# A two-layer decoder on one core: LayerNorm means moved into centred weights, scales into the evacuations, of the third many-head stage

## The reference, cut to what matters

```python
def _ln(x, g, b, eps=1e-05):
    m = jnp.mean(x, -1, keepdims=True)
    var = jnp.mean((x - m) ** 2, -1, keepdims=True)
    return (x - m) * jax.lax.rsqrt(var + eps) * g + b
def _proj(x, g, b, W, bias):
    return _ln(x, g, b) @ W.T + bias
...
qh = split_heads(_proj(q, ln_q_w, ln_q_b, w_q, b_q))
kh = split_heads(_proj(k, ln_k_w, ln_k_b, w_k, b_k))
vh = split_heads(_proj(v, ln_v_w, ln_v_b, w_v, b_v))
...
return _proj(o, ln_o_w, ln_o_b, w_o, b_o)
```

## Time and profile before

| what | us |
| --- | --- |
| median of 3 runs | 926.53 (925.84 to 928.22) |
| the profiled execution's own time | 924.71 |
| its span, first to last instruction | 922.9 |
| TensorE busy | 859.1 (93%) |
| VectorE busy | 549.8 (60%) |
| ScalarE busy | 423.1 (46%) |
| GpSimd busy | 234.9 (25%) |

### The profile page before, as it was taken

One profiled execution on the slowest core, in us unless ns is written; L12 is line 12 of the kernel. 1 busy time (PEld: TensorE's weight loads), 2 busy tenths in 40 slices (PEclk: granted clock), 3 DMA queues, 4 the chain that ended last, 5 costly groups with the idle time before them and its releaser, 6 DMA issues.

```text
span 922.9 us, 16788 instructions
## 1 busy us (share of the span) xinstructions
PE 859.1 (93%) x6416; PEld 703.1 (76%) x6416; DVE 549.8 (60%) x1371; ACT 423.1 (46%) x1226; POOL 234.9 (25%) x351
## 2 busy tenths in 40 slices
PE   3889999997999999999999998999989999999998
PEld 3777777775878888777777676777757888888887
DVE  2566777776322212777778776777755555555554
ACT  1335666655322232666665566666775312222211
POOL 2112113121241112332244556666600000000000
PEclk9999999999999999999999999999989999999999
DMA  8700000000000000000010000000000000000000
GB/s 332 304 1 12 25 13 13 13 24 1 1 1 1 1 1 1 1 1 2 1 36 36 13 13 12 13 1 2 2 1 2 11 1 13 12 12 12 12 12 11
DMA packets 8733, 22.51 MB, mean 24 GB/s; under 512 B 1360, under 2 KB 3664, under 8 KB 7504
## 3 DMA queue, kind: packets, MB, share of 16 engines
q1 hardware_dynamic: 8656, 21.46, 6.3%
HBM read 19.35 MB, written 2.10 MB: 23 GB/s over the span
## 4 chain that ended last, share of the span: by engine, by line
PE 74%; ACT 13%; DVE 10%; issue 1%; DMA 1%; SPq 0%; POOL 0%; DVEq 0%; POOLq 0%; ACTq 0%
PE sc L552 15%; ACT pr L1078 8%; PE pj L372 8%; PE pj L283 7%; PE pj L290 7%; PE ov L448 6%; PE sc L435 6%; PE sc L361 5%; DVE mx L776 5%; PE ov L562 4%; PE pj L562 4%; PE pj L277 3%; PE sc L356 3%; PE ov L383 2%; PE ov L290 2%; PE pj L392 1%
## 5 line engine op out<-in xcount | busy, mean ns | idle before, releaser
L1078 ACT ACTIVATE pr<-sc,mx 128x128 f32<-128x128 f32 x768 | 217.2, 411 | 118.1 <-DVE mx L776 118.0
L776 DVE TENSOR_REDUCE mx<-sc 128x4 f32<-128x512 f32 x192 | 119.2, 683 | 50.2 <-PE sc L361 50.2
L372 PE MATMUL pj<-idn,pr 128*128 128x128 f32 x768 | 121.1, 281 | 24.1 <-ACT pr L1078 12.0
L783 DVE COPY pT<-pj 128x512 f32<-128x512 f32 x160 | 108.7, 686 | 35.1 <-PE pj L372 33.9
L372 PEld LDWEIGHTS pj<-idn,pr 128*128 128x128 f32 x768 | 87.3, 142 | 53.1 <-issue 17.6
L1225 POOL TENSOR_SCALAR ve<-mv 128x2 f32<-128x2 f32 x40 | 8.9, 222 | 412.8 <-DVE mv L722 412.8
L1116 ACT ACTIVATE sh<-sc 128x256 f32<-128x256 f32 x80 | 30.7, 384 | 155.7 <-PE sc L552 155.7
L1096 ACT ACTIVATE hT<-sc,vecs 128x256 f32<-128x256 f32 x64 | 30.4, 474 | 90.2 <-PE sc L435 90.2
L552 PE MATMUL sc<-xnT,W 128*128 128x256 f32 x256 | 66.2, 381 | 0.0
L552 PE MATMUL sc<-xnT,Wup 128*128 128x256 f32 x256 | 65.7, 379 | 0.0
L435 PE MATMUL sc<-xnT,W 128*128 128x256 f32 x256 | 64.1, 380 | 0.0
(11 more groups left out here) (171 smaller groups left out, 1575.8 us busy)
## 6 DMA issues: line engine op xcount, KB each, us to landing
cT<-in_ctxT SPq DMA_DIRECT2D x8, 256.0 KB, 3.1
W<-in_w SPq DMA_DIRECT2D x2, 1024.0 KB, 13.5
cT<-in_ctx SPq DMA_DIRECT2D x8, 256.0 KB, 2.6
out_x<-X SPq DMA_DIRECT2D x8, 256.0 KB, 2.0
X<-in_x SPq DMA_DIRECT2D x1, 1792.0 KB, 9.1
rws<-in_rows SPq DMA_DIRECT2D x1, 1064.0 KB, 11.6
hT<-in_tokk SPq DMA_DIRECT2D x1, 1024.0 KB, 11.0
Wx<-in_w_x SPq DMA_DIRECT2D x1, 1024.0 KB, 16.1
```

The source lines that it names most:

```text
L372: last = tr(bank[b][:, i * S:(i + 1) * S], pr[n % 4][:, i, :], idn[:])
L776: v.tensor_reduce(mx[n % 4][:], four(b), AX.X, ALU.max, negate=True).then_inc(mx_done, 1)
L783: v.tensor_copy(pT[n % 4][:], four(b)).then_inc(drained[b], 1)
L1078: last = a(pr[n % 4][:, i, :], bank[b][:, i * S:(i + 1) * S], ACT.Exp, bias=mx[n % 4][:, i:i + 1])
```

## The change

For stage 4 the mean is no longer subtracted from the data. At unit 20 (`FOLD + 2`) four products of a matrix of ones with the scaled weights (`center(i)`) give the column sums of each weight matrix, and VectorE subtracts the column means (`centered(i)`, two instructions each). The projection of raw data with centred weights equals that of centred data. The inverse deviation of each token is a per-partition scalar at the evacuation: `biased`, `values` and `residual` of stage 4 become two `scalar_tensor_tensor` instructions each, one for each sequence, of 128x256, in place of one `tensor_tensor` of 128x512. `ctx_norm`, `head_norm` and the `x_norm` of stage 4's units are gone; so are `turn_context` and its ScalarE copy: the context is loaded already turned (`ctxT`). Its statistics still need the context by tokens; `ctx_stats` moves to stage 2 (unit 16 + p) with its loads, and the SP queue reloads `cT` for stage 4. `turn_x` of stage 4 transposes X itself; the bias add to X (`x_plus`) waits for that. The heads are turned raw one unit earlier: `turn_heads(U - 1)` in `part2` instead of `turn_heads4(U - 2)` in `part0`, and so is ScalarE's copy of it. In all attention units, of stages 1 and 3 too, VectorE's `alone0` and `alone1` come behind the part and the copy of the half's first transposed probabilities instead of ahead of the part.

```diff
+            def center(i):
+                b, n = begin("pj", "center", i)
+                pe.wait_ge(drained[b], n - 1)
+                pe.wait_ge(s_folded, i + 1)
+                for c in range(C):
+                    last = mm(bank[b][:, 0:D], ones[:], Wx[:, i, c, :], start=c == 0, stop=c == C - 1)
+                last.then_inc(filled[b], 1)
...
+            def centered(i):
+                b, n = spot["center", i]
+                dve.wait_ge(filled[b], n)
+                for c in range(C):
+                    last = v.scalar_tensor_tensor(Wx[:, i, c, :], bank[b][:, 0:D], -1.0 / D, Wx[:, i, c, :],
+                                                  ALU.mult, ALU.add)
+                last.then_inc(drained[b], 1)
...
             def biased(W, i):
...
-                v.tensor_tensor(rt[:, i], twice(b), over(bias4[:, i, :], 2), ALU.add).then_inc(drained[b], 1)
+                for j in two:
+                    last = v.scalar_tensor_tensor(rt[:, i, j, :], bank[b][:, j * D:(j + 1) * D], scale[:, j:j + 1],
+                                                  bias4[:, i, :], ALU.mult, ALU.add)
+                last.then_inc(drained[b], 1)
...
-                pe.wait_ge(*emptied("cT", W))
-                along_tokens(b, cnT[W % 2], Wx[:, 1])
+                pe.wait_ge(s_ct[W % 2], 64 + 16 * (W % PAIRS // 2 + 1))
+                along_tokens(b, cT[W % 2], Wx[:, 1])
...
+                if stage(W) == 4:
+                    pe.wait_ge(*emptied("o", W - PAIRS))
+                    turn_pair(b, xp(W % PAIRS))
...
-                if stage(U - 2) == 4:
-                    turn_heads4(U - 2)
...
-                if stage(U + 2) == 4:
-                    turn_context(U + 2)
-                if stage(U - 1) == 3:
-                    turn_heads3(U - 1)
+                if stage(U - 1) in (3, 4):
+                    turn_heads(U - 1)
...
                 dense(U, 2 * j)
-                (alone0, alone1)[j](U)
+                if f not in ATT:
+                    (alone0, alone1)[j](U)
                 (part0, part2)[j](U)
                 if f in ATT:
                     copy_probs(U, 4 * j)
+                    (alone0, alone1)[j](U)
                 dense(U, 2 * j + 1)
...
             def alone0(U):
                 if stage(U + 2) is not None:
                     x_stats(U + 2)
-                if stage(U + 2) == 4:
-                    ctx_norm(U + 2)
+                if stage(U) == 2:
+                    ctx_stats(U % PAIRS)
 
             def alone1(U):
-                if stage(U - 1) == 4:
-                    head_norm(U - 1)
-                if stage(U + 2) is not None:
+                if stage(U + 2) in (0, 1, 2, 3, 5):
                     x_norm(U + 2)
```

More of the change, by code:

```diff
@@ L143, in program @@
         cbst = sb("cbst", [P, 2, 6])
-        cmv = [sb(f"cmv{r}", [P, 2, 2]) for r in two]
+        cmv = [sb(f"cmv{p}", [P, 2, 2]) for p in range(PAIRS)]
         cve = sb("cve", [P, 2])
-        crs = [sb(f"crs{r}", [P, 2]) for r in two]
-        cn = [Wq0[:], Wk0[:]]
+        crs = [sb(f"crs{p}", [P, 2]) for p in range(PAIRS)]
         cnT = [sb(f"cnT{r}", [P, C, T]) for r in two]
@@ L151, in program @@
         hst = sb("hst", [P, 2, 6])
-        hmv = sb("hmv", [P, 2, 2])
+        hmv = [sb(f"hmv{r}", [P, 2, 2]) for r in two]
         hve = sb("hve", [P, 2])
-        hrs = sb("hrs", [P, 2])
-        hn = Wqk[:]
+        hrs = [sb(f"hrs{r}", [P, 2]) for r in two]
+        ones = sb("ones", [P, P])
         hdT = [lnbs[:].rearrange("p i c s -> p (i c s)")[:, r * C * T:(r + 1) * C * T].rearrange("p (c t) -> p c t", c=C)
@@ L644, in part1 @@
                     fold(1)
+                if U == FOLD + 2:
+                    center(1)
                 if attends(U):
@@ L663, in part2 @@
                     fold(2)
+                if U == FOLD + 2:
+                    center(2)
             def part3(U):
@@ L681, in part3 @@
                     fold(3)
+                if U == FOLD + 2:
+                    center(3)
                 if attends(U):
@@ L701, in _ @@
                 if U == 4 * PAIRS - 2:
-                    pe.wait_ge(s_folded, 4)
+                    for i in range(4):
+                        pe.wait_ge(*emptied("center", i))
                     pe.wait_ge(s_mb, 2)
@@ L809, in residual @@
                 dve.wait_ge(xadd, PAIRS * (f - 2) + p + 1)
-                v.tensor_tensor(xp(p), twice(b), xp(p), ALU.add).then_inc(drained[b], 1)
+                if f == 4:
+                    dve.wait_ge(hrs_done, p + 1)
+                    for j in two:
+                        last = v.scalar_tensor_tensor(xs(p, j), bank[b][:, j * D:(j + 1) * D], hrs[p % 2][:, j:j + 1],
+                                                      xs(p, j), ALU.mult, ALU.add)
+                    last.then_inc(drained[b], 1)
+                else:
+                    v.tensor_tensor(xp(p), twice(b), xp(p), ALU.add).then_inc(drained[b], 1)
             def router_logits(W):
@@ L965, in part0 @@
                     unfolded(0)
+                if U == FOLD + 2:
+                    centered(0)
             def part1(U):
@@ L983, in part1 @@
                     unfolded(1)
+                if U == FOLD + 2:
+                    centered(1)
                 if attends(U):
@@ L993, in part2 @@
                     unfolded(2)
+                if U == FOLD + 2:
+                    centered(2)
             def part3(U):
@@ L1007, in part3 @@
                     unfolded(3)
+                if U == FOLD + 2:
+                    centered(3)
                 if attends(U):
                     copy_probs(U, 7)
-                if stage(U + 3) == 4:
-                    ctx_stats(U + 3)
             def alone0(U):
@@ L1257, in x_plus @@
                 f, p = W // PAIRS, W % PAIRS
-                pool.wait_ge(xn_done, W + 1)
+                if f == 4:
+                    pool.wait_ge(mv_done, W + 1)
+                    pool.wait_ge(*full("xT", W))
+                else:
+                    pool.wait_ge(xn_done, normed(W))
                 if f == 3:
@@ L1363, in _ @@
                 else:
-                    sp.wait_ge(cn_done, p - 1)
+                    sp.wait_ge(cst_done, p - 1)
+                sp.dma_start(cx[p % 2][:], ctx[:, 2 * p:2 * p + 2, :]).then_inc(s_cx[p % 2], 16)
+            for p in range(PAIRS):
+                if p < 2:
+                    sp.wait_ge(cst_done, PAIRS - 1 + p)
+                else:
+                    sp.wait_ge(*full("v", 4 * PAIRS + p - 2))
                 if p == 2:
```

88 lines of the change are left out of this document (45 added, 43 removed).

## The result

The changed kernel has a median of 919.52 us (918.35 to 920.96, 4 runs), the kernel before beside it 926.34 us (925.84 to 928.22, 4 runs): ratio 0.9923, 95% interval 0.9904 to 0.9943. The forecast was 925.2, "the same". The profiled execution took 918.35 us with a span of 916.4, 6.5 less than before.

| kernel | median us | ratio to the kernel before of the same occasion | 95% interval |
| --- | --- | --- | --- |
| changed, first | 919.52 (4 runs) | 0.9923 | 0.9904 to 0.9943 |
| changed, second | 921.55 (12) | 0.9977 | 0.9964 to 0.999 |
| changed, third | 920.93 (12) | 0.9968 | 0.9953 to 0.9983 |
| before, second | 923.53 (12) | 0.9993 | 0.9978 to 1.0007 |
| before, third | 922.52 (10) | 0.9987 | 0.9971 to 1.0002 |

What follows compares the result with a forecast made beforehand. TensorE, busy 93% of the span, was taken as the bound, then its waits around stage 4. Terms -6.6 - 3.2 - 0.9 + 4.1 + 5.3 = -1.3 took the median from 926.5 to 925.2 us, range 919.4 to 930.

Steps and rivals of the forecast that it cites:

- units 34–37: Steady units of stage 4: first halves gain 1.80 us, net -1.65 a unit, -6.6 us over four units.
- units 30–33: Four units lose four turns of a context or the wait for it: -3.2 us in sum.
- units 38, 39 and stage 5: Unit 38 unchanged, unit 39 one copy less (-0.5), stage 5 one turn fewer (-0.4): together -0.9 us.
- stage 1: Second halves: `x_norm` moved behind the first copy delays later copies for which TensorE waits: +4.1 us, bounds 0 to 5.2.
- stage 2: Unit 20: four centring products and a late residual cost +5.3 us; lower bound 3.4, the products alone.
- stage 3: VectorE's same move falls into a wait for the output product of over a microsecond: 0.
- the new stall of pT2: First halves of units 34 to 37: pT2 waits for its bank, which `values` empties late, about 0.45 us.
- Rival 3: Slower: the `scalar_tensor_tensor` pairs stretch beside GpSimd to between 1.35 and 1.97 us; 933 us at the least; chance 0.07.
- Rival 1: VectorE's order costs nothing in stage 1, as copies have slack: 921.1 us, 919.4 without the clock's fall; chance 0.25.
- Rival 4: Stage 4's stall moves whole from `value4` to pT1 or pT2; a unit gains only 0.44: 930.0 us; chance 0.10.
- Its edges: The forecast's step for units around the steady ones: -3.2 us for units 30 to 33, -0.9 for later parts.
- Rival 2: The clock doesn't fall in unit 33, as `key4` waits less: -3.0 us in all, 923.5 us; chance 0.15.

Runs made afterwards that it cites:

- e1: The changed kernel with VectorE's `alone0` and `alone1` put back ahead of the part in every attention stage: 913.68 us, ratio 0.9894.
- e2: The kernel before with only the new order of VectorE's calls: 928.09 us, ratio 1.0056.
- e7: The changed kernel with `turn_context` and ScalarE's copy put back, their result unused by the projections: 929.7 us, ratio 1.0056.
- e3: The changed kernel with the new order of VectorE's calls kept in stage 4 only: 915.48 us, ratio 0.9921.

## Why the prediction was wrong

| step | forecast | first trace less first before | without what chance gives |
| --- | --- | --- | --- |
| units 34–37 | -6.6 | -6.90 | -6.9 |
| units 30–33 | -3.2 | -6.29 | -4.6 |
| units 38, 39 and stage 5 | -0.9 | -0.86 | -0.9 |
| stage 1 | +4.1 | +3.64 | +3.7 |
| stage 2 | +5.3 | +5.17 | +5.2 |
| stage 3 | 0 | +0.60 | +0.6 |
| start | 0 | -1.86 | 0 |
| sum | -1.3 | -6.50 | -2.9 |

The last column compares the second trace of the changed kernel with the third of the kernel before (clock whole in unit 33, stage 1's last half short in both), but for units 38, 39 and stage 5, where it keeps the first pair: other pairs of the traces give between -1.1 and +0.6 there. Its -2.9 is 0.31% of 924: the ratios 0.9977 and 0.9968 of the later occasions say 0.23 and 0.32%. The means of all three traces of either kernel, from the first scores of stage 1 to the end of the span, are 841.5 and 844.6 us, 3.1 apart.

**Right.** First halves 9.77 (9.84 forecast), second halves 10.97 (11.0), the new stall of pT2 0.33 (0.45), pT6 +0.19 (+0.15), the pairs 0.88 and 0.84, unit 20 at 21.42 (21.5), stage 1's second halves 8.85 (8.9). Rival 3 is out: the pair at 593.71 ran at 0.84 with GpSimd at work from 593.57 to 594.98. The rule of the Trainium skill, SBUF — State Buffer, section Who interferes with whom, under which such a pair stays clear of the shared port, agrees with that row. Rival 1 is out: stage 1 pays, and e1 gives it back. Rival 4 is out, though e2 shows it true in the main for the order alone: there 1.0 of the 1.56 us wait stood at the next evacuation.

**Right in the half's length, wrong in what it was owed to.** The forecast let `biased` come early because the new order puts it right behind the maxima, and took the new stall of pT2 as the price. e1 puts the old order back, and the halves get 0.23 us shorter (9.54), without that stall. Nor do the loads stay "as before": the changed kernel issues 16 turned ones in place of 8 beside the 8 by tokens, 24.61 MB in all against 22.51. The 0 that the forecast gives them holds: the view of its waits lists none of TensorE that ends with a load.

**Wrong, the forecast as a whole: "the 924.71 becomes 923.4".** Two parts.

The sum itself was 1.6 too small a gain. The step that failed is "Its edges", -3.2 for units 30 to 33. The four units gave (before, third trace, to changed): 0.62, 1.89, 1.12 and 0.98 against my 0.59, 1.19, 0.6 and 0.75. What I missed lies in the second halves of units 31 and 32, 0.55 each. Unit 32 in the third trace of the kernel before:

```profile
530.60 0.66 PE L277 MATMUL pj<-idn,hT 128*128 128x128 f32 x4
531.09 0.60 PE L277 MATMUL pj<-idn,Wq 128*128 128x128 f32 x4
531.53 0.60 PE L277 MATMUL pj<-idn,hd 128*128 128x128 f32 x4
...
533.60 0.66 PE L372 MATMUL pj<-idn,pr 128*128 128x128 f32 x4 [1.47 <-ACT qT L1064]
...
534.18 1.96 PE L290 MATMUL pj<-Wx,cnT 128*128 128x256 f32 x8
```

and in the changed kernel:

```profile
536.30 0.65 PE L280 MATMUL pj<-idn,hT 128*128 128x128 f32 x4
536.79 0.60 PE L280 MATMUL pj<-idn,hd 128*128 128x128 f32 x4
...
537.39 0.63 PE L379 MATMUL pj<-idn,pr 128*128 128x128 f32 x4
...
539.31 1.99 PE L293 MATMUL pj<-Wx,cT 128*128 128x256 f32 x8 [1.29 <-ACT qT L1101]
```

Three turns fill the ring before, pT4 is its fourth use and stands behind the queries' copy, `key4` behind pT4. With two turns pT4 takes the third bank and runs inside the wait; `key4` is the one that waits, and starts 5.09 us after the half's scores (534.22) instead of 5.67 after them (528.51). e7 bears this out: it puts the context's turn and its copy back, and the second halves of units 31 and 32 get 0.50 and 0.49 us longer (12.77 and 12.44 against 12.27 and 11.95). I had counted the turn's 0.44 in units 30 and 32 only as TensorE's time and had not moved the ring along in the units that have no output product ahead of pT4. Against this, stage 3's 0.6 was missing ("in stage 3 the same move falls into a wait": e1 and e3, which undo it there, return to 115.7 and 115.6), and stage 1 was 0.4 too dear.

The rest of the first difference isn't shown to be in the change. The step that failed here is the level: I took the 924.71 us to subtract from, but it holds a clock fall of 1.68 us, and its stage 1 starts 1.86 us later than in the changed kernel's first trace. Neither is fixed to its kernel: the fall is in one trace of three, and the start is 76.40 to 77.79 in four traces of the kernel before and of e2, 75.48 to 78.12 in ten of the changed kernel and its variants. Rival 2 had the fall (chance 0.15), but as a thing that the change removes; the repetitions show that the kernel before has it in one trace of three. The two together are 3.5 of the first traces' 6.5.

**Left open.** The first occasion's medians differ by 6.8 us, the later ones by some 2 to 4 (ratios whose intervals do not meet: at most 0.9943, and at least 0.9953). The four first runs before took 925.84 us and more, which even the profiled execution, with its clock fall and its late start, did not reach (924.71); of the 58 runs of the kernel before that stand beside the later ones only 7 did. The times go with the clock. Each of the 58 has its mean granted clock on record: the 15 with 0.993 or more took 922.3 us on average, none over 923.41; the 43 with less took 924.5, and all 7 are among these. For the four first runs no clock is on record, so how much of their time was clock stays open, and so does whether the chip mattered, which is on record only for the later occasions (11 for the changed kernel's second run, 0 for the rest).

## What to carry to other kernels

When a tile's use of a ring leaves or comes, write the ring's order anew for every unit of the pattern, the first and last ones too, and ask of each use which evacuation it waits for: the same turn of 0.44 us was worth 1.67 us at one place and 0.58 at another. When an instruction that held a queue up is removed, the reordering that was made around it should be tried undone: here the removal gave the gain and the new order lost some 6 us of it, so that the old order with a later centring is 8 us faster than the change. And before a forecast within 0.3% is made from one profile, look for places in it where the clock fell: what they cost may be missing in the next execution of the same kernel.

## What the runs showed of the hardware

- The granted clock fell or stayed whole at the same place of the same kernel, behind the same wait of 1.87 us: 0.66 over 5 us in one execution, so part of it at 1.2 in place of 2.4 GHz, and whole in two (1.00 over 553.80 to 565.00 and over 551.06 to 562.20 us), where the eight matmuls took 1.97 us. The price was 1.68 us. At the end of stage 1 the last half differed by 1.37 us in the same way (11.86 us with a granted clock of 1.00 and 13.23 with 0.74, one kernel).
- A `scalar_tensor_tensor` pair with one operand in PSUM kept 0.84 us while GpSimd worked on SBUF tensors; the `tensor_scalar` pairs with both ends in SBUF had ranged from 0.73 to 1.97.
- The start, up to the first scores of stage 1, varied by 2.6 us (75.48 to 78.12) over the 14 traces, and the landing of its 1792 KB load with it (7.4 to 9.9 us after the issue). Unedited, one kernel gave 75.48 to 76.97, the other 76.40 to 77.79.
- Whole executions of the kernel before spread from 920.66 to 928.22 us, and the shorter ones had the higher granted clock: 922.3 us on average at 0.993 or more, 924.5 below, in the 58 runs beside the later ones.
